# Splitting the second product of a conditional residual kernel differently: one matmul per sample and half instead of three per pair and half

## The chip, the cores and the metric

The kernel runs on one core of a Trainium2 chip. Its time is the device time of that core in microseconds (us). Of the kernel before there are three timed runs, and one profiled execution from which the trace comes.

## The reference

```python
x = x + einsum('bct,bcd->bdt', x, L0_cond_weights[itok_B_0_15])     # 64 x 64 per sample
x = x + einsum('bsi,boi->bso', x, L1_cond_weight[itok_B_3_7])       # 1024 x 1024 per sample
```

x is 128 samples of 64 x 1024 in float32. The first index picks one of 16 matrices W0 of 64 x 64, the second one of 8 adapters of 1024 x 1024 (the indices drawn are 3 to 7, so five adapters are used). Both steps are of the form (1 + W) applied to x, from the left and from the right, so they can be done in either order.

## The kernel before

The kernel does the large product first, z = x (1 + W1), and then y = (1 + W0) z. Two samples of one adapter make a pair of 128 rows, and a pair is one **slot**; an adapter with an odd number of samples has a last slot with one sample. There are 66 slots, numbered s, in groups of one adapter each. A table made on the chip says which samples, which W0s and which adapter a slot has.

Numbers are kept in fp32r, a rounded float32 that TensorE multiplies at full rate, and every factor is split into hi (the rounded value) and lo (what the rounding dropped), so that a product takes three matmuls: hi by hi, hi by lo, lo by hi. A slot has these steps:

- x is loaded by 8 DMAs (queue of SP), and VectorE (DVE) turns its 32 x 32 blocks (`turn_x`, L794). ScalarE (ACT) makes xt_hi (L572), DVE xt_lo (L803). In a slot with one sample, xt_hi holds hi in one half and lo in the other (L807).
- TensorE (PE) sums z in two halves of 512 columns, each half 8 tiles by 3 matmuls of 512 columns (`sum_z`, L467, L468, L470). Slots use the banks z_ps and first_ps by turns.
- ACT makes z_hi of a half (L584), DVE z_lo (L819), each 128 x 512.
- PE makes y of a half with 3 matmuls (`sum_y`, L481 to L483) whose stationary matrix is a block-diagonal w0_parts: W0 of sample A in one corner (put there by ACT, L580), W0 of sample B in the other (put there by DVE, L815). A slot with one sample uses w0_twice instead (L579).
- ACT copies y out of PSUM (L589) and issues the stores (L596).

The adapter of the next group is brought in meanwhile: it consists of 8 chunks of 128 rows, and the first 8 slots of a group handle one chunk each. A chunk is loaded, gets the identity added on GpSimd (L275), is turned by DVE (L779), and ACT and DVE make w_hi (L568) and w_lo (L789) of it. I call a slot with such a chunk a chunk slot and the others free slots. There are four groups that fetch a next one, hence 32 chunk slots.

Every engine has its own program, a loop over slots, and the engines meet at semaphores. In PE's program the y of slot s-1 stands between the two halves of z of slot s. ACT and DVE work strictly in the order of their programs. In DVE's program a slot s is, before the change:

```python
turn_x(j + h, 1 - h)        # x of slot s+1
keep_xt_lo(s + 1, 1 - h)    # waits for ACT's xt_hi, which waits for turn_x
turn_chunks(first, last)    # a chunk: turn, wait for ACT's w_hi, w_lo
keep_z_lo(s, h, 0)
place_w0_b(s)
keep_z_lo(s, h, 1)
```

`look` (L206) loads fields of the slot's row of the table into registers, on the engine that needs them.

## Time and profile before

| | us |
|---|---|
| median of 3 runs (lowest, highest) | 830.72 (828.99, 831.37) |
| profiled execution, its own time | 828.85 |
| its span | 827.1 |
| PE busy | 808.9 (98%) |
| DVE busy | 448.7 (54%) |
| ACT busy | 279.2 (34%) |
| GpSimd busy | 23.4 (3%) |

PE's matmuls are pipelined: each row of one lasts 0.39 us, but a new one starts every 0.227 us. Busy is the time in which at least one instruction of an engine runs. The time outside the span, 1.75 us, belongs to the start and the end of the execution. The trace also has rows for the sequencers (PEq, DVEq, ACTq), which do the loads into registers, the branches and the waits.

### The profile page before, as it was taken

What the parts mean: (1) busy time and instruction counts of PE and PEld (TensorE: products, weight loads), DVE (VectorE), ACT (ScalarE), POOL (GpSimd) and SP (SyncE); (2) the same over time, 40 slices, a digit from 0 to 9 for tenths busy, and PEclk for the clock granted to TensorE, in tenths of its full rate; (3) what the DMA queues carried; (4) which work ended last, traced back from release to release, by engine and by line L of the source; (5) the groups of instructions that cost most, each with busy time, mean ns of one, the idle gap of its engine ahead of it and who ended that gap; (6) DMA issues with size and microseconds to landing.
All of it is one profiled execution on the core that took longest, in us unless ns stands there. A gap on an engine that the chain in (4) does not pass through costs nothing.

```text
span 827.1 us, 17869 instructions
## 1 busy us (share of the span) xinstructions
PE 808.9 (98%) x3580; PEld 669.5 (81%) x3581; DVE 448.7 (54%) x472; ACT 279.2 (34%) x515; POOL 23.4 (3%) x60
## 2 busy tenths in 40 slices
PE   4999999999999999999999999999999999999998
PEld 4888888788888888888888888888888888888886
DVE  6666666566765434666663466665443343343342
ACT  3323424333333323424333233333332332332232
POOL 1100000010000000000000000000000000000000
PEclk9999999999999999999999999999999999999999
DMA  6344343444433324444333444433332233232232
GB/s 212 105 119 151 121 140 96 126 128 139 138 104 88 98 79 121 124 146 122 109 101 83 119 122 145 129 106 95 93 101 61 89 94 83 77 101 78 75 101 76
DMA packets 73952, 90.88 MB, mean 110 GB/s; under 512 B 13780, under 2 KB 64468, under 8 KB 73940
## 3 DMA queue, kind: packets, MB, share of 16 engines
q1 hardware_dynamic: 63616, 57.45, 23.2%
q10 hardware_dynamic: 10324, 33.30, 15.2%
q14 instruction: 8, 0.07, 0.0%
q8 instruction: 4, 0.07, 0.0%
HBM read 57.15 MB, written 33.55 MB: 110 GB/s over the span
## 4 chain that ended last, share of the span: by engine, by line
PE 82%; DVE 5%; issue 2%; ACT 2%; DVEq 2%; ACTq 1%; SPq 1%; DMA 1%; POOL 0%; POOLq 0%
PE z_ps L467 12%; PE first_ps L467 12%; PE z_ps L468 12%; PE first_ps L468 12%; PE z_ps L470 12%; PE first_ps L470 11%; PE y_ps L481 3%; PE y_ps L482 3%; PE y_ps L483 3%; DVE w_turned L779 2%; DVE x_turned L794 2%; DVEq L206 1%; ACT xt_hi L572 1%; ACT w_hi L568 1%; DMA w_nat<-in_L_cond_weight_dram 1%
## 5 line engine op out<-in xcount | busy, mean ns | idle before, releaser
L467 PE MATMUL z_ps<-w_hi,xt_hi 128*128 (+1 forms) x528 | 205.6, 389 | 0.5 <-DVE xt_lo L803 0.5
L468 PE MATMUL z_ps<-w_lo,xt_hi 128*128 (+1 forms) x528 | 205.4, 389 | 0.0
L467 PE MATMUL first_ps<-w_hi,xt_hi 128*128 x528 | 205.4, 389 | 0.0
L468 PE MATMUL first_ps<-w_lo,xt_hi 128*128 x528 | 205.4, 389 | 0.0
L470 PE MATMUL z_ps<-w_hi,xt_lo 128*128 (+1 forms) x512 | 199.2, 389 | 0.0
L470 PE MATMUL first_ps<-w_hi,xt_lo 128*128 x480 | 186.7, 389 | 0.0
L794 DVE STREAM_TRANSPOSE x_turned<-x_in 128x1024 f32<-128x1024 f32 x66 | 141.5, 2144 | 26.2 <-issue 23.3
L572 ACT ACTIVATE xt_hi<-x_turned 128x1024 fp32r<-128x1024 f32 x66 | 70.0, 1061 | 234.1 <-DVE x_turned L794 229.1
L803 DVE TENSOR_TENSOR xt_lo<-x_turned,xt_hi 128x1024 fp32r<-128x1024 f32 x61 | 74.8, 1225 | 78.4 <-ACT xt_hi L572 78.4
L467 PEld LDWEIGHTS z_ps<-w_hi,xt_hi 128*128 128x128 f32 x528 | 99.1, 188 | 21.7 <-issue 0.9
L467 PEld LDWEIGHTS first_ps<-w_hi,xt_hi 128*128 128x128 f32 x528 | 99.1, 188 | 20.7
L468 PEld LDWEIGHTS first_ps<-w_lo,xt_hi 128*128 128x128 f32 x528 | 99.1, 188 | 20.3
L468 PEld LDWEIGHTS z_ps<-w_lo,xt_hi 128*128 128x128 f32 x528 | 99.1, 188 | 20.3
L470 PEld LDWEIGHTS z_ps<-w_hi,xt_lo 128*128 128x128 f32 x512 | 96.1, 188 | 20.1
L470 PEld LDWEIGHTS first_ps<-w_hi,xt_lo 128*128 128x128 f32 x480 | 90.1, 188 | 18.8
L819 DVE TENSOR_TENSOR z_lo<-z_ps,z_hi 128x512 fp32r<-128x512 f32 x66 | 45.5, 689 | 89.3 <-ACT z_hi L584 88.0
L819 DVE TENSOR_TENSOR z_lo<-first_ps,z_hi 128x512 fp32r<-128x512 f32 x66 | 45.5, 689 | 88.4 <-ACT z_hi L584 88.0
L789 DVE TENSOR_TENSOR w_lo<-w_turned,w_hi x32 | 39.3, 1227 | 72.7 <-ACT w_hi L568 72.7
L568 ACT ACTIVATE w_hi<-w_turned x32 | 34.0, 1062 | 123.1 <-DVE w_turned L779 123.1
L589 ACT ACTIVATE y<-y_ps 128x512 f32<-128x512 f32 x130 | 70.2, 597 | 0.0
L779 DVE STREAM_TRANSPOSE w_turned<-w_nat 128x1024 f32<-128x1024 f32 x32 | 68.3, 2134 | 0.4 <-POOL w_nat L275 0.4
L584 ACT ACTIVATE z_hi<-z_ps 128x512 fp32r<-128x512 f32 x66 | 39.1, 593 | 84.9 <-PE z_ps L470 68.0
(137 smaller groups left out, 418.0 us busy)
## 6 DMA issues: line engine op xcount, KB each, us to landing
x_in<-in_x_dram SPq DMA_DIRECT2D x536, 64.0 KB, 2.0
out_dram<-y ACTq DMA_DIRECT2D x126, 256.0 KB, 3.1
w_nat<-in_L_cond_weight_dram SPq DMA_DIRECT2D x128, 128.0 KB
w_nat<-in_L_cond_weight_dram SPq DMA_DIRECT2D x4, 512.0 KB, 5.5
w_turned<-in_L_cond_weight_dram SPq DMA_DIRECT2D x2, 512.0 KB, 5.9
y<-in_L_cond_weight_dram SPq DMA_DIRECT2D x2, 512.0 KB, 8.1
x_turned<-in_L_cond_weights_dram SPq DMA_DIRECT2D x2, 256.0 KB, 4.0
x_in<-in_x_dram SPq DMA_DIRECT2D x2, 256.0 KB, 6.3
```

The source lines that it names most:

```text
L467: nc.tensor.matmul(to, xt_hi[h][:, t, :], whi, start=(t == 0), stop=False)
L468: mm = nc.tensor.matmul(to, xt_hi[h][:, t, :], wlo, start=False, stop=last and not pair)
L470: mm = nc.tensor.matmul(to, xt_lo[h][:, t, :], whi, start=False, stop=last)
L568: nc.scalar.activation(of_chunk(w_hi, k), turned(k), ACT.Copy).then_inc(chunk_hi_made, 1)
L572: nc.scalar.activation(xt_hi[h][:], x_turned[h][:], ACT.Copy).then_inc(xt_hi_made, 1)
L584: nc.scalar.activation(z_hi[:, n], z_banks[h][n][:], ACT.Copy).then_inc(z_hi_made, 1)
L589: nc.scalar.activation(y[h][:, n * HALF:(n + 1) * HALF], y_ps[n][:], ACT.Copy).then_inc(y_made, 1)
L779: nc.vector.transpose(w_turned[:, q].rearrange("p (t b m) -> p b t m", b=BLOCKS, m=BLOCK), w_nat[:, q].rearrange("p (b m t) -> p b t m", b ...
L789: nc.vector.tensor_tensor(of_chunk(w_lo, k), turned(k), of_chunk(w_hi, k).bitcast(F32), ALU.subtract).then_inc(chunk_lo_made, 1)
L794: nc.vector.transpose(x_turned[h][:].rearrange("p t (b m) -> p b t m", m=BLOCK), x_in[h][:].rearrange("p (b m t) -> p b t m", b=BLOCKS, m= ...
L803: nc.vector.tensor_tensor(xt_lo[h][:], x_turned[h][:], xt_hi[h][:].bitcast(F32), ALU.subtract).then_inc(xt_lo_made, 1)
L819: nc.vector.tensor_tensor(z_lo[:, n], z_banks[h][n][:], z_hi[:, n].bitcast(F32), ALU.subtract).then_inc(z_lo_made, 1)
```

## The change

z's hi and lo parts of one sample are stacked over the 128 partitions, and W0's hi and lo parts are set side by side as 128 columns, so that a single matmul of a sample and a half gives all the products. Its result has the part of W0's hi in 64 rows and that of W0's lo in the other 64, and these two are added afterwards: ACT copies one over to the other's partitions, DVE adds. The banks of y double from two to four, and one pair of start-up banks goes. DVE's slot is put in another order: the chunk is turned first, beside x, and x of slot s+2 is turned between the two halves.

```diff
-        w0_parts = sb("w0_parts", [P, 2, P], F32R)
-        w0_twice = sb("w0_twice", [P, 2, C], F32R)
-        z_hi = sb("z_hi", [P, NH, HALF], F32R)
-        z_lo = sb("z_lo", [P, NH, HALF], F32R)
+        w0_parts = sb("w0_parts", [P, 2, 2 * C], F32R)
+        z_parts = sb("z_parts", [P, NH, 2, HALF], F32R)
...
-        y_ps = [bank(f"y_ps{n}") for n in range(NH)]
+        y_ps = [[bank(f"y_ps{n}{k}") for k in range(2)] for n in range(NH)]
...
@@ SP, at the start @@
-            for c in range(6):
+            for c in range(4):
                 load_first(c)
-            sp.wait_ge(table_made, 1)
+            sp.wait_ge(samples_made, 1)
...
@@ PE @@
             def sum_y(s, pair):
...
                 for n in range(NH):
-                    pe.wait_ge(z_lo_made, NH * s + n + 1)
-                    to = y_ps[n][0:rows]
-                    nc.tensor.matmul(to, w0_slot[:, 0], z_hi[:, n], start=True, stop=False)
-                    nc.tensor.matmul(to, w0_slot[:, 0], z_lo[:, n], start=False, stop=False)
-                    nc.tensor.matmul(to, w0_slot[:, 1], z_hi[:, n], start=False, stop=True).then_inc(y_summed, 1)
+                    for k in range(2):
+                        pe.wait_ge(w0_placed, 2 * s + k + 1)
+                        pe.wait_ge(z_lo_made, PER_Z * s + 2 * n + k + 1)
+                        mm = nc.tensor.matmul(y_ps[n][k if pair else 0][:], w0_parts[:, k], z_parts[:, n, k],
+                                              start=pair or k == 0, stop=pair or k == 1)
+                        mm.then_inc(y_summed, 1)
...
                     if not second:
-                        pe.wait_ge(y_made, NH * before)
+                        pe.wait_ge(y_made, PER_Y * before)
                     sum_y(before, pair)
...
@@ ACT @@
             def keep_z_hi(s, h, n):
                 act.wait_ge(z_summed, NH * s + n + 1)
-                nc.scalar.activation(z_hi[:, n], z_banks[h][n][:], ACT.Copy).then_inc(z_hi_made, 1)
+                for k in range(2):
+                    nc.scalar.activation(z_parts[rows_of(k), n, k], z_banks[h][n][rows_of(k)],
+                                         ACT.Copy).then_inc(z_hi_made, 1)
+
+            def place_w0(s):
+                for k, cond in enumerate(look(act, s, COND_A, COND_B)):
+                    nc.scalar.activation(w0_parts[:, k], own_w0(cond), ACT.Copy).then_inc(w0_placed, 1)
+
+            def begin_y(s, h, stored):
+                act.wait_ge(y_stored[h], stored + STORED_AHEAD)
+                def across(k, n, count):
+                    act.wait_ge(y_summed, PER_Y * s + 2 * n + 2)
+                    nc.scalar.activation(y[h][rows_of(k), n * HALF:(n + 1) * HALF], y_ps[n][k][rows_of(1 - k)],
+                                         ACT.Copy).then_inc(y_begun, count)
+                stores, = look(act, s, STORES)
+                with act.If(stores > 1):
+                    for n in range(NH):
+                        for k in range(2):
+                            across(k, n, 1)
+                with act.Else():
+                    for n in range(NH):
+                        across(0, n, 2)
...
             def slot(j, h, before, stored):
...
                 keep_z_hi(s, h, 0)
-                make_y(before, 1 - h)
-                place_w0_a(s)
+                act.wait_ge(y_summed, PER_Y * before + 4)
+                place_w0(s)
+                begin_y(before, 1 - h, stored)
                 keep_z_hi(s, h, 1)
                 store_y(before, 1 - h)
...
@@ DVE @@
             def keep_z_lo(s, h, n):
-                dve.wait_ge(z_hi_made, NH * s + n + 1)
-                nc.vector.tensor_tensor(z_lo[:, n], z_banks[h][n][:], z_hi[:, n].bitcast(F32), ALU.subtract).then_inc(z_lo_made, 1)
+                for k in range(2):
+                    dve.wait_ge(z_hi_made, PER_Z * s + 2 * n + k + 1)
+                    nc.vector.tensor_tensor(z_parts[rows_of(1 - k), n, k], z_banks[h][n][rows_of(k)],
+                                            z_parts[rows_of(k), n, k].bitcast(F32), ALU.subtract).then_inc(z_lo_made, 1)
+
+            def finish_y(s, h):
+                def add(k, n, begun, count):
+                    dve.wait_ge(y_begun, PER_Y * s + begun)
+                    own = y[h][rows_of(k), n * HALF:(n + 1) * HALF]
+                    nc.vector.tensor_tensor(own, y_ps[n][k][rows_of(k)], own, ALU.add).then_inc(y_made, count)
...
-            def slot(j, h):
+            def slot(j, h, before):
                 s = 2 * j + h
                 first, last = look(dve, s, CHUNKS_BEFORE, CHUNKS)
-                turn_x(j + h, 1 - h)
+                with dve.If(last > first):
+                    turn_chunk(first)
                 keep_xt_lo(s + 1, 1 - h)
-                turn_chunks(first, last)
+                with dve.If(last > first):
+                    keep_chunk_lo(first)
+                with dve.If(last > first + 1):
+                    with dve.Fori(first + 1, last) as k:
+                        turn_chunk(k)
+                        keep_chunk_lo(k)
                 keep_z_lo(s, h, 0)
-                place_w0_b(s)
+                finish_y(before, 1 - h)
+                turn_x(j + 1, h)
                 keep_z_lo(s, h, 1)
```

On DVE, from the first z_lo of a slot in the loop to the turning of the next x, this stood before:

```order
L819 TENSOR_TENSOR z_lo<-z_ps,z_hi 128x512
L206 ISA
L206 TENSOR_LOAD slot_row
L815 ISA
L815 COPY w_parts<-w_all 64x2x64
L818 REGISTER_ALU
L819 TENSOR_TENSOR z_lo<-z_ps,z_hi 128x512
L206 ISA
L206 TENSOR_LOAD slot_row
L793 ISA
L794 STREAM_TRANSPOSE x_turned<-x_in 128x4x8x32
```

From the same place, up to the second of four sums of y, DVE now has:

```order
L808 TENSOR_TENSOR z_parts<-z_ps,z_parts 64x512
L807 REGISTER_ALU
L808 TENSOR_TENSOR z_parts<-z_ps,z_parts 64x512
L205 ISA
L205 TENSOR_LOAD slot_row
L819 COMPARE_AND_BRANCH
L814 ISA
L816 TENSOR_TENSOR y<-y_ps,y 64x512
L814 REGISTER_ALU
L816 TENSOR_TENSOR y<-y_ps,y 64x512
```

Each z_lo has become two instructions on 64 partitions, the copy of W0 has left DVE, and a load of a field, a branch and four sums of y have come between the z_lo of the first half and the turning of x, which for its part stands ahead of the z_lo of the second half.

On PE, the y of a slot with two samples was this:

```order
L481 MATMUL y_ps<-z_hi,w_parts 128x512
L482 MATMUL y_ps<-z_lo,w_parts 128x512
L483 MATMUL y_ps<-z_hi,w_parts 128x512
L481 MATMUL y_ps<-z_hi,w_parts 128x512
L482 MATMUL y_ps<-z_lo,w_parts 128x512
L483 MATMUL y_ps<-z_hi,w_parts 128x512
```

It is now this, in the same place between the halves of z:

```order
L479 MATMUL y_ps<-z_parts,w_parts 128x512
L477 REGISTER_ALU
L478 REGISTER_ALU
L479 MATMUL y_ps<-z_parts,w_parts 128x512
L478 REGISTER_ALU
L479 MATMUL y_ps<-z_parts,w_parts 128x512
L478 REGISTER_ALU
L479 MATMUL y_ps<-z_parts,w_parts 128x512
```

Six matmuls of 512 columns have become four of 512 columns, and each of the four waits for a z_lo of its own.

## Rows read from the trace of the kernel before

**Rows 1.** Part 1 of the page: busy time of each engine.
```profile
PE 808.9 (98%) x3580; PEld 669.5 (81%) x3581; DVE 448.7 (54%) x472; ACT 279.2 (34%) x515; POOL 23.4 (3%) x60
```

**Rows 2.** Waits of PE: line, waited for, us in total, times, longest.
```profile
PE first_ps L448 <- DMA x_in<-in_x_dram: 3.4, 1, 3.4
...
PE z_ps L467 <- DVE xt_lo L803: 0.5, 1, 0.5
```

**Rows 3.** Stretches: busy us (instructions) of each engine, granted clock, DMA.
```profile
22.00:24.00 2.00, 1.64 (x8) 1.64 (x9) 0.00 (x0) 0.49 (x1) 1.36 (x6) 0.50 0.86 311
...
574.30:821.00 246.70, 246.70 (x1090) 203.96 (x1089) 99.31 (x102) 73.84 (x145) 0.00 (x0) 1.00 0.32 85
```

**Rows 4.** DVE's turnings of chunks, line L779: durations, and busy tenths in 40 slices.
```profile
L779 DVE STREAM_TRANSPOSE w_turned<-w_nat x32: 2112/2130/2161, 46.0 to 562.0; 128x1024 f32<-128x1024 f32 x32
...
busy tenths in 40 slices 0021221012111000221210022111000000000000
```

**Rows 5.** DVE in order of time, one chunk slot and parts of its neighbours.
```profile
411.93 0.68 DVE L819 TENSOR_TENSOR z_lo<-first_ps,z_hi 128x512 fp32r<-128x512 f32 x1
412.64 0.23 DVE L815 CAST w_parts<-w_all 64x128 fp32r x1
412.97 0.69 DVE L819 TENSOR_TENSOR z_lo<-first_ps,z_hi 128x512 fp32r<-128x512 f32 x1
414.29 2.15 DVE L794 STREAM_TRANSPOSE x_turned<-x_in 128x1024 f32<-128x1024 f32 x1 [0.63 <-issue]
417.57 1.23 DVE L803 TENSOR_TENSOR xt_lo<-x_turned,xt_hi 128x1024 fp32r<-128x1024 f32 x1 [1.13 <-ACT xt_hi L572]
418.71 2.12 DVE L779 STREAM_TRANSPOSE w_turned<-w_nat 128x1024 f32<-128x1024 f32 x1
423.03 1.23 DVE L789 TENSOR_TENSOR w_lo<-w_turned,w_hi  x1 [2.20 <-ACT w_hi L568]
424.17 0.68 DVE L819 TENSOR_TENSOR z_lo<-z_ps,z_hi 128x512 fp32r<-128x512 f32 x1
...
425.21 0.69 DVE L819 TENSOR_TENSOR z_lo<-z_ps,z_hi 128x512 fp32r<-128x512 f32 x1
426.00 2.15 DVE L794 STREAM_TRANSPOSE x_turned<-x_in 128x1024 f32<-128x1024 f32 x1
```

**Rows 6.** ACT in order of time, in the same slot.
```profile
421.36 1.06 ACT L568 ACTIVATE w_hi<-w_turned  x1 [3.83 <-DVE w_turned L779]
...
422.80 1.08 ACT L589 ACTIVATE y<-y_ps 128x512 f32<-128x512 f32 x2
...
423.96 0.30 ACT L580 ACTIVATE w_parts<-w_all 64x128 fp32r x1
```

**Rows 7.** Two neighbours on DVE without a change of partitions.
```profile
133.12 0.69 DVE L807 TENSOR_TENSOR xt_hi<-x_turned,xt_hi 128x512 fp32r<-128x512 f32 x1 [1.13 <-ACT xt_hi L572]
133.73 2.16 DVE L779 STREAM_TRANSPOSE w_turned<-w_nat 128x1024 f32<-128x1024 f32 x1
```

**Rows 8.** DVE's loads of table fields into registers: durations in ns, min/median/max.
```profile
L206 DVEq TENSOR_LOAD <-slot_row x198: 300/318/1864, 20.8 to 816.0; - x198
```

**Rows 9.** Slot 1: PE's first matmul; DVE's first chunk turned.
```profile
39.10 0.39 PE L467 MATMUL first_ps<-w_hi,xt_hi 128*128 x1
...
46.05 2.13 DVE L779 STREAM_TRANSPOSE w_turned<-w_nat 128x1024 f32<-128x1024 f32 x1 [0.35 <-POOL w_nat L275]
```

**Rows 10.** The end, in order of time: PE's last z, then ACT and DVE.
```profile
820.86 0.39 PE L470 MATMUL first_ps<-w_hi,xt_lo 128*128 x1
...
821.28 0.60 ACT L584 ACTIVATE z_hi<-first_ps 128x512 fp32r<-128x512 f32 x1 [4.07 <-PE first_ps L470]
...
821.91 0.69 DVE L819 TENSOR_TENSOR z_lo<-first_ps,z_hi 128x512 fp32r<-128x512 f32 x1 [5.08 <-ACT z_hi L584]
...
823.19 0.69 DVE L859 COPY y<-y_ps 128x512 f32<-128x512 f32 x1 [0.59 <-PE y_ps L542]
```

More of the change, by code:

```diff
@@ L183, in conditional_residual_kernel @@
         w0_lo_made = sem("w0_lo_made")
-        w0_placed = [sem(f"w0_placed{k}") for k in range(2)]
+        w0_placed = sem("w0_placed")
         z_summed = sem("z_summed")
@@ L359, in _ @@
                 sp.dma_start(x_in[0][k * C:(k + 1) * C, :], x_rows[bass.ds(sample * C, C), :]).then_inc(x0_loaded, 16)
-            for c in range(6, CHUNKS_PER_GROUP):
+            for c in range(4, CHUNKS_PER_GROUP):
                 load_first(c)
@@ L530, in y_last @@
             def y_last(pair):
-                pe.wait_ge(y_made, 4 * pairs_past + 2)
-                s = 2 * pairs_past + 1
-                for k in range(2):
-                    pe.wait_ge(w0_placed[k], s + 1)
-                w0_slot, rows = (w0_parts, P) if pair else (w0_twice, C)
-                for n in range(NH):
-                    to = y_ps[n][0:rows]
-                    pe.wait_ge(z_hi_made, NH * s + n + 1)
-                    nc.tensor.matmul(to, w0_slot[:, 0], z_hi[:, n], start=True, stop=False)
-                    nc.tensor.matmul(to, w0_slot[:, 1], z_hi[:, n], start=False, stop=False)
-                    pe.wait_ge(z_lo_made, NH * s + n + 1)
-                    nc.tensor.matmul(to, w0_slot[:, 0], z_lo[:, n], start=False, stop=True).then_inc(y_summed, 1)
+                pe.wait_ge(y_made, PER_Y * (2 * pairs_past + 1))
+                sum_y(2 * pairs_past + 1, pair)
             for_both(stores, y_last)
@@ L598, in store_y @@
                 with act.If(stores > 1):
-                    act.wait_ge(y_made, NH * s + NH)
+                    act.wait_ge(y_made, PER_Y * s + PER_Y)
                     store(a, 0)
@@ L607, in store_y, with slot @@
                     with act.Else():
-                        act.wait_ge(y_made, NH * s + NH)
+                        act.wait_ge(y_made, PER_Y * s + PER_Y)
                         act.sem_inc(y_stored[h], 32)
-            def slot(j, h, before, last_of_all=False):
+            def slot(j, h, before, stored):
                 s = 2 * j + h
@@ L771, in keep_x0_lo, with turn_chunk, turn, keep_chunk_lo @@
                     keep(slice(C, P), xt_hi[0])
-            def turn_chunks(first, last):
-                with dve.If(last > first):
-                    with dve.Fori(first, last) as k:
-                        def turn(q):
-                            dve.wait_ge(chunk_with_1, k + 1)
-                            nc.vector.transpose(
-                                w_turned[:, q].rearrange("p (t b m) -> p b t m", b=BLOCKS, m=BLOCK),
-                                w_nat[:, q].rearrange("p (b m t) -> p b t m", b=BLOCKS, m=BLOCK)
-                                ).then_inc(chunk_turned, 1)
-                        with dve.If(k % 2 < 1):
-                            turn(0)
-                        with dve.Else():
-                            turn(1)
-                        dve.wait_ge(chunk_hi_made, k + 1)
-                        nc.vector.tensor_tensor(of_chunk(w_lo, k), turned(k), of_chunk(w_hi, k).bitcast(F32),
-                                                ALU.subtract).then_inc(chunk_lo_made, 1)
+            def turn_chunk(k):
+                def turn(q):
+                    dve.wait_ge(chunk_with_1, k + 1)
+                    nc.vector.transpose(
+                        w_turned[:, q].rearrange("p (t b m) -> p b t m", b=BLOCKS, m=BLOCK),
+                        w_nat[:, q].rearrange("p (b m t) -> p b t m", b=BLOCKS, m=BLOCK)
+                        ).then_inc(chunk_turned, 1)
+                with dve.If(k % 2 < 1):
+                    turn(0)
+                with dve.Else():
+                    turn(1)
+            def keep_chunk_lo(k):
+                dve.wait_ge(chunk_hi_made, k + 1)
+                nc.vector.tensor_tensor(of_chunk(w_lo, k), turned(k), of_chunk(w_hi, k).bitcast(F32),
+                                        ALU.subtract).then_inc(chunk_lo_made, 1)
             def turn_x(j, h):
@@ L821, in slot @@
-            def slot(j, h):
+            def keep_z_lo(s, h, n):
+                for k in range(2):
[7 more added lines that the diff above has]
+                    nc.vector.tensor_tensor(own, y_ps[n][k][rows_of(k)], own, ALU.add).then_inc(y_made, count)
+                stores, = look(dve, s, STORES)
+                with dve.If(stores > 1):
+                    for n in range(NH):
+                        for k in range(2):
+                            add(k, n, 2 * n + k + 1, 1)
+                with dve.Else():
+                    for n in range(NH):
+                        add(0, n, 2 * n + 2, 2)
```

95 lines of the change are left out of this document (34 added, 61 removed).

## The prediction

> **What bounds the kernel now.** First the busy shares [rows 1]: PE is busy 98% of the span, the next engine, DVE, 54%. Then PE's waits [rows 2]: behind the start there is one, 0.5 us long, for DVE's xt_lo. Then the pace [rows 3]: in the undisturbed stretch at the end PE starts 1090 matmuls in 246.7 us, one per 0.2263 us, at full granted clock. So the time is the number of matmuls of 512 columns by 0.2265 us: a slot has 48 of z and 6 of y, 54 x 0.2265 = 12.23 us.
>
> The average of 54% on DVE hides two sorts of slots. In a chunk slot DVE goes from one turning of x (414.29) to the next (426.00) in 11.7 us, and from z_lo at 411.93 to z_lo at 424.17 in 12.24 us, with next to no spare time [rows 5]: of this it waits 1.13 us for xt_hi and 2.20 us for w_hi, answers from ACT that come only after its own turnings. The wait of PE for xt_lo stands at the end of the first series of 8 such slots. The chunk slots come in four series of 8, 32 turnings [rows 4]. DVE is thus already a near second bound in them, and the change adds to DVE.
>
> **PE, what it saves.** y of a slot takes 4 matmuls where it took 6, for pairs and for single samples alike, with the same 512 columns and, since the stationary matrix still has 128 columns, the same pace. All 66 slots: 396 become 264. I count the last slot in the tail; the other 65 save 130 x 0.2265 = **29.4 us**. A slot needs 52 x 0.2265 = 11.78 us of PE.
>
> **ACT, what it gets.** Two more passes of z_hi and two more of y, each 0.49 us behind another (1.08 us for two [rows 6]), so some 2 us a slot on an engine that is busy a third of the time [rows 1]. Cover: in a chunk slot ACT sits idle 3.83 us before w_hi [rows 6]. Without the cover it would cost up to 2 us in each slot. I take 0. Its stores are issued behind the last of y as before.
>
> **DVE, what it gets.** Gone: the copy of W0, 0.23 us. Added in a pair slot: two z_lo passes and four sums of y, all of 512 columns, 0.69 us each, since half the partitions save nothing: the copy of 64 partitions [rows 5] is short by its 128 columns. In the new order xt_lo needs no wait, as its x was turned in the slot before, and it fills 1.2 us of the 2.2 us in which DVE waits for w_hi. Laid end to end from the start of the last z_lo of a chunk slot to that of the next:
>
> - to the turning of the chunk: 0.79 us in the first slot of the loop's body and 1.32 us past the loop's end [rows 5], mean 1.05, and two more branches and a wait, for which I put 0.2: 1.25
> - from the turning to w_lo: 4.32 [rows 5], xt_lo inside it
> - w_lo to z_lo: 1.14 overlapped as before, 1.26 if it may not overlap: 1.26
> - z_lo to z_lo 0.72, z_lo to the first sum of y 0.72 (the load of one field, 0.32 [rows 8], lies beside), three more sums 2.16, last sum to the turning of x 0.72
> - the turning of x to z_lo 2.18, z_lo to z_lo 0.72
>
> Sum **14.05 us**, against 11.78 us of PE. The spacing of the seven short steps is the choice that matters. A pass of 0.69 us is followed after 0.61 us in one place [rows 7], and after 0.71 us in the other, where the next one begins at another partition (z_lo, then the copy to rows 64 on [rows 5]). Nearly every new instruction changes between rows 0 and 64 in what it reads or writes, so I take 0.72. At 0.61 throughout, with 1.14 for w_lo and without the 0.2, the chain is 12.9 us; with 0.1 more on each step for register work it is 14.9 us.
>
> The Trainium skill has a rule on this (VectorE: DVE Perf Modes, section "Two Vector instructions with no wait between them"): an instruction whose inputs or output start in another quadrant of partitions than those before is held until everything earlier has finished. By that rule every z_lo, every sum of y and both turnings here are held, which is the chain of 14.05 us; without it the sum would come out at 828 us as in the second case below. The two spacings agree with it.
>
> **How far DVE may fall behind.** In free slots PE sets the pace. The end of z gives the offsets [rows 10]: last matmul starts at 820.86, so PE is through at E = 821.08; z_hi starts at E+0.2, z_lo at E+0.83. In the new order DVE is by then still turning x: ACT makes z_hi twice, two W0s and four copies, so the last sum of y ends at about E-0.5, the turning at E+1.6, and the second z_lo starts at E+2.3. PE needs it at E + 24 + 3 matmuls = E+6.1, minus 0.75 for the pass: E+5.3. Slack: **3.0 us**. A chunk slot uses up 14.05 - 11.78 = 2.27 us of it, and what remains is a wait of PE before y. It isn't won back, since in free slots PE can do no better than 11.78.
>
> - Series 2 to 4: 8 x 2.27 - 3.0 = 15.2 us each, 45.5 us. The free slots between (at least two) give DVE some 1.8 us each, enough to restore the slack.
> - Series 1 starts without slack: DVE turns the first chunk at 46.05, when it has landed, with slot 1 on PE since 39.10 [rows 9], some 0.5 earlier after. From there 4.32+1.26+0.72+0.72+2.16+0.72+2.18+0.72 brings the second z_lo to 58.9, needed at 38.6 + 11.78 + 5.3 = 55.7: 3.2 late, and 7 more slots by 2.27: 19.1 us. The 0.5 us of before [rows 2] goes into this.
>
> **Start.** x of slot 0 is asked for ahead of two chunks instead of behind. PE waited 3.4 us for it [rows 2]. The bytes ahead of the last chunk are the same, and PE would wait for chunks next: between 0 and 3.4, I take 0.5 us of gain, near the lower end because of the DMA load in that stretch [rows 3].
>
> **Tail.** Before, the last copy on DVE starts 2.1 us after E [rows 10]. After: z_lo twice (E+0.83 and 1.5), the last matmul at E+2.2, its end 0.4 later, two copies on ACT of 0.6 and 0.5, the last sum at E+4.0: **+1.9 us**.
>
> **Sum**, against the profiled execution's own 828.85 us: - 29.4 - 0.5 (start) - 0.5 (old wait) + 45.5 + 19.1 + 1.9 = 865.0. The median of the runs is 1.9 us above that execution; I halve that and say **866 us**.
>
> **The rivals.**
> 1. DVE's steps overlap, chain 12.9 us. For it: [rows 7]. Series 2 to 4 cost 8 x 1.12 - 3.0 = 6.0 each, series 1 2.3 + 7 x 1.12 = 10.1: 28.1 in all, 828 us, no change. With chains from 12.3 to 13.4 us this case spans 809 to 844.
> 2. Faster: DVE keeps pace. The place is the wait for w_hi: if ACT's answer came while xt_lo runs, turning to w_lo would be 2.13 + 1.23 = 3.4 us instead of 4.32, and the chain 11.95 us with overlap. That is below the 12.15 us from which 8 slots use up the slack. Only some 3 us of series 1 stay: 803 us. Against it: ACT starts w_hi 0.5 us after the turning ends, needs 1.06, and DVE starts 0.6 later [rows 5, 6]. The change is a gain at all only below a chain of some 12.9 us.
> 3. Worse: a wait not in the chain (sums of y waiting for ACT's copies, loads into registers, the longest of which took 1.86 us [rows 8]), chain 15 us or more: 895 us.
>
> TensorE's clock is no case of its own. After the 3.4 us wait for x the granted clock was 0.50, its 1.2 GHz level [rows 2, 3]. PE's new waits are some 2.3 us a slot, and should the clock fall nonetheless, what the slower matmuls lose comes out of PE's wait for DVE.
>
> **How the numbers follow.** Forecast (chains of 13.4 to 14.9 us, 844 to 892) 0.67, rival 1 0.18, rival 2 0.10, rival 3 0.05. The range that leaves out rival 2, the lower end of rival 1 and the top is 826 to 884. A measurement here tells 0.3%, 2.5 us, from no change. Faster: rival 2 and a third of rival 1, 0.16; same 0.05; slower 0.79.
>
> **What would show it.** Right: four blocks of PE waits for z_lo inside the series of 8, some 2.3 us a slot from the second slot on, none in free slots; DVE near 100% busy or waiting for w_hi there, slots of 14 us; y at 4 matmuls of 0.2265; DVE busy about 66 x 3.9 us more. Wrong: PE waits in free slots, or for y_made, or waits for w_hi of under 0.5 us, or PE without waits at a span near 800.

## The result, and the profile after

The changed kernel took **858.25 us** (median of four executions, 857.83 to 859.58), the kernel before 831.05 us on the same chip (828.99 to 831.84). The ratio is 1.0327, with a 95% interval of 1.031 to 1.0343: 3.3% slower. The profiled execution of the changed kernel took 859.58 us, with a span of 857.6; before it was 828.85 with a span of 827.1. So there are 30.5 us to find inside the span. In all that follows one execution stands apart: of the ten of the kernel with the new order and the old y, one took 1674.46 us and the others 829.93 to 831.99, and its ratio leaves that one out.

Part 1 of the changed kernel's page is the counterpart of [rows 1]:

```profile
PE 806.3 (94%) x3448; PEld 644.7 (75%) x3449; DVE 706.1 (82%) x795; ACT 453.3 (53%) x771; POOL 23.7 (3%) x59
```

132 matmuls are gone, and yet PE is busy for only 2.6 us less: a matmul that is held up by the next one's input is drawn longer than its 0.23 us, so part of the waiting hides in "busy". DVE has gained 257 us, which is 66 slots by 3.9 us. At 82% it still doesn't look like a bound; the average is over slots with and without a chunk.

PE's waits, the counterpart of [rows 2]:

```profile
PE y_ps L479 <- DVE z_parts L808: 30.5, 54, 1.9
...
PE y_ps L448 <- DMA x_in<-in_x_dram: 1.3, 1, 1.3
PE y_ps L479 <- DVE y L816: 0.9, 2, 0.6
```

Where before there was one wait of 0.5 us behind the start, there are now 54 waits before y for z_lo (L808), and two for sums of y. Nearly all stand where the chunks are turned (DVE's L771, the counterpart of [rows 4]: its first and last start, and in which of the 40 slices it is busy):

```profile
L771 DVE STREAM_TRANSPOSE w_turned<-w_nat x32: 2120/2186/2242, 47.1 to 595.1; 128x1024 f32<-128x1024 f32 x32
...
busy tenths in 40 slices 0021212021212000112120011212000000000000
```

How long a slot is, I read from PE's starts, from the first matmul after one y to the first after the next. Before, it was 12.24 us in every slot of two samples, but for the one wait. Now it is 11.78 to 11.79 us in most slots without a chunk, and 13.5 to 13.7 us in those with one, apart from the first one or two of a series (15.39 us in the first series, where the chunk comes late, and 11.8 to 12.3 us in the others, where the slack is used up first). Here is one slot with a chunk on DVE, in order of time, to be laid beside [rows 5] (start, duration, line, operation, count, and in brackets the idle time before it and who ended it):

```profile
390.83 2.15 DVE L771 STREAM_TRANSPOSE w_turned<-w_nat 128x1024 f32<-128x1024 f32 x1
392.91 1.18 DVE L797 TENSOR_TENSOR xt_lo<-x_turned,xt_hi 128x1024 fp32r<-128x1024 f32 x1
395.25 1.23 DVE L783 TENSOR_TENSOR w_lo<-w_turned,w_hi  x1 [1.16 <-ACT w_hi L555]
396.51 1.41 DVE L808 TENSOR_TENSOR z_parts<-z_ps,z_parts 64x512 fp32r<-64x512 f32 x2
397.95 2.85 DVE L816 TENSOR_TENSOR y<-y_ps,y 64x512 f32<-64x512 f32 x4
400.83 2.13 DVE L788 STREAM_TRANSPOSE x_turned<-x_in 128x1024 f32<-128x1024 f32 x1
403.00 1.41 DVE L808 TENSOR_TENSOR z_parts<-z_ps,z_parts 64x512 fp32r<-64x512 f32 x2
404.43 2.17 DVE L771 STREAM_TRANSPOSE w_turned<-w_nat 128x1024 f32<-128x1024 f32 x1
```

From turning to turning it is 404.43 - 390.83 = 13.60 us; over the seven steps of the first series it is (142.66 - 47.14)/7 = 13.65. Only the 1.16 us before w_lo are idle, and not one instruction of this slot waits for PE. PE for its part, at the start of this stretch, waits for the z_lo of the slot before: its second half has two, which DVE starts at 389.39 and 390.11, and PE waits for each:

```profile
388.70 0.61 PE L479 MATMUL y_ps<-z_parts,w_parts 128*128 128x512 f32 x2
390.13 0.50 PE L479 MATMUL y_ps<-z_parts,w_parts 128*128 128x512 f32 x1 [0.82 <-DVE z_parts L808]
390.86 0.49 PE L479 MATMUL y_ps<-z_parts,w_parts 128*128 128x512 f32 x1 [0.22 <-DVE z_parts L808]
391.37 0.49 PE L467 MATMUL z_ps<-w_hi,xt_hi 128*128 x1
```

From 388.70 to 391.37 four matmuls take 2.67 us; at the usual pace they would take 0.91. The brackets show only 1.04 of this loss, since the ends of the held matmuls are drawn late. So the list of waits (30.5 us) understates the loss, and I count by starts.

**The books of the span, before to after:**

| where | predicted, us | measured, us |
|---|---|---|
| y with four matmuls for six | -29.4 | -29.0 (64 slots by 0.453) |
| old wait for xt_lo, and start | -1.0 | -0.8 |
| first series of chunks | +19.1 | +20.3 |
| waits in the other three | +45.5 | +35.0 (11.8, 11.6, 11.7) |
| behind single-sample slots | 0 | +1.0 |
| tail | +1.9 | +4.1 |
| sum | +36.1 | +30.6, of 30.5 |

A row's loss is what its slots take beyond 11.785 us (9.98 where a slot has one sample).

Not all of the 20.3 us are waits. Behind the last chunk slot of the first series comes a slot in which PE waits for nothing, and still it takes 1.7 us too long. In it eight matmuls start 0.43 us apart instead of 0.227, because the granted clock is down at 0.50, the 1.2 GHz level (PE, PEld, DVE, ACT, GpSimd, then the clock, DMA's share and GB/s):

```profile
158.00:161.00 3.00, 3.00 (x9) 2.35 (x8) 2.88 (x5) 2.68 (x6) 0.00 (x0) 0.50 0.32 89
```

PE had lost 3.7 us in the slot before. In the kernel below whose sums have 256 columns, where the clock stays at 1.00, the same slot loses 0.6 us, so the fall costs here at least 1.1 us, by my estimate.

### The profile page after: what moved, and what is told of

It reads as the page before. It is cut to its first block, busy times and chain, and to the rows that moved or that the text cites. A ratio compares the mean times of both kernels' runs of the same rounds, so it can differ in the third digit from the quotient of the medians.

```text
span 857.6 us, 19195 instructions
## 1 busy us (share of the span) xinstructions
PE 806.3 (94%) x3448; PEld 644.7 (75%) x3449; DVE 706.1 (82%) x795; ACT 453.3 (53%) x771; POOL 23.7 (3%) x59
## 4 chain that ended last, share of the span: by engine, by line
PE 40%; DVE 22%; issue 17%; DVEq 10%; ACT 5%; ACTq 2%; DMA 2%; SPq 1%; POOL 0%; POOLq 0%
DVE w_turned L771 8%; DVE z_parts L808 8%; PE z_ps L467 6%; PE first_ps L467 6%; PE z_ps L470 6%; PE z_ps L468 6%; PE first_ps L468 6%; DVEq L205 5%; PE first_ps L470 5%; DVE y L816 5%; ACT w_hi L555 4%; PE y_ps L479 3%; DVEq L783 2%; ACTq L555 2%; DMA y<-in_L_cond_weight_dram 1%
## 5 line engine op out<-in xcount | busy, mean ns | idle before, releaser
L467 PE MATMUL first_ps<-w_hi,xt_hi 128*128 x528 | 208.2, 394 | 0.3
L816 DVE TENSOR_TENSOR y<-y_ps,y 64x512 f32<-64x512 f32 x256 | 176.0, 689 | 16.8 <-ACT y L577 9.7
L577 ACT ACTIVATE y<-y_ps 64x512 f32<-64x512 f32 x256 | 150.7, 590 | 7.5 <-PE y_ps L479 2.5
L788 DVE STREAM_TRANSPOSE x_turned<-x_in 128x1024 f32<-128x1024 f32 x67 | 143.5, 2142 | 2.0
L479 PE MATMUL y_ps<-z_parts,w_parts 128*128 128x512 f32 x264 | 87.1, 416 | 31.7 <-DVE z_parts L808 30.5
L468 PEld LDWEIGHTS first_ps<-w_lo,xt_hi 128*128 128x128 f32 x528 | 99.7, 189 | 20.3
L564 ACT ACTIVATE z_parts<-z_ps 64x512 fp32r<-64x512 f32 x132 | 78.2, 592 | 44.7 <-PE z_ps L470 31.2
L564 ACT ACTIVATE z_parts<-first_ps 64x512 fp32r<-64x512 f32 x132 | 78.2, 593 | 43.7 <-PE first_ps L470 29.3
L808 DVE TENSOR_TENSOR z_parts<-z_ps,z_parts 64x512 fp32r<-64x512 f32 x132 | 90.9, 689 | 9.2 <-ACT z_parts L564 5.3
L808 DVE TENSOR_TENSOR z_parts<-first_ps,z_parts 64x512 fp32r<-64x512 f32 x132 | 90.9, 689 | 9.0 <-ACT z_parts L564 5.2
```

The source lines that it names most:

```text
L467: nc.tensor.matmul(to, xt_hi[h][:, t, :], whi, start=(t == 0), stop=False)
L468: mm = nc.tensor.matmul(to, xt_hi[h][:, t, :], wlo, start=False, stop=last and not pair)
L479: mm = nc.tensor.matmul(y_ps[n][k if pair else 0][:], w0_parts[:, k], z_parts[:, n, k], start=pair or k == 0, stop=pair or k == 1)
L564: nc.scalar.activation(z_parts[rows_of(k), n, k], z_banks[h][n][rows_of(k)], ACT.Copy).then_inc(z_hi_made, 1)
L577: nc.scalar.activation(y[h][rows_of(k), n * HALF:(n + 1) * HALF], y_ps[n][k][rows_of(1 - k)], ACT.Copy).then_inc(y_begun, count)
L788: nc.vector.transpose(x_turned[h][:].rearrange("p t (b m) -> p b t m", m=BLOCK), x_in[h][:].rearrange("p (b m t) -> p b t m", b=BLOCKS, m= ...
```

## The experiments

The theory: in a slot with a chunk, DVE's steps laid end to end (the chain, 13.65 us) are longer than PE's 11.79, and after some 3 us of slack each such slot costs PE the difference. The rivals: a wait or register work that the list of steps doesn't hold, or the new order of DVE's slot. All kernels from here on except the changed one itself carry this addition in `look`, by which the values loaded from the table are kept in bounds:

```diff
-            return values
+            return tuple(eng.snap(v & (TOP[f] | 7), min_val=0, max_val=TOP[f]) if f in (GROUP, CHUNKS_BEFORE, CHUNKS) else v
+                         for f, v in zip(range(fields[0], fields[-1] + 1), values))
```

**The addition alone**, on the changed kernel. It adds register instructions ahead of DVE's turnings, so it is a test of the register rival too.

> The changed kernel, with the table's chunk and group fields masked to their range (value & 63, value & 7) after each load: what the runs below are compared with. One or two register operations more for each load of these fields. If DVE's sequencer has time to spare beside the passes, as the chain theory has it (the steps behind the loads follow without a gap in the changed kernel's trace, 0.72 us from z_lo to the turning of the chunk), the slot stays at 13.65 us and the time at 858 us within 2. If register work is what sets the chain, each of 31 slots gets some 0.1 us longer: 861 us or more.

Measured: 859.51 us (856.76 to 860.24), ratio 1.0325 (1.030 to 1.0351). The chain stayed at 13.63 to 13.66 us (the mean of each series), and the turning of the chunk still starts 0.72 us after the last z_lo. More register work there costs nothing that can be measured: it runs while the pass before it does. This kernel is the base for the experiments below.

**Less of each sum of y.** The four sums stay four instructions but get fewer columns, 256 or 64 for 512. The rest of y is left out.

```diff
-                    own = y[h][rows_of(k), n * HALF:(n + 1) * HALF]
-                    nc.vector.tensor_tensor(own, y_ps[n][k][rows_of(k)], own, ALU.add).then_inc(y_made, count)
+                    own = y[h][rows_of(k), n * HALF:n * HALF + 256]
+                    nc.vector.tensor_tensor(own, y_ps[n][k][rows_of(k), 0:256], own, ALU.add).then_inc(y_made, count)
```

> The four sums of y take 256 of their 512 columns; the other columns of the output lack the part of one of W0's halves. Chain theory: a pass of 256 columns is 0.27 us shorter, the chain of a chunk slot 13.65 - 1.07 = 12.58 us, PE loses 8 x 0.80 - 3.3 = 3.1 us in series 2 to 4 and about 9 in series 1: 55 - 18 = 37 us less, about 822. Rival, the hand-over between PE, ACT and DVE costs PE the time (each wait a matter of latency, not of DVE's work): the number of hand-overs is unchanged, 855 to 860.

> The four sums of y take 64 of their 512 columns; the rest of the output's columns lack one part. Chain theory: 0.47 us less on each of four passes, chain 11.8 us, as long as PE's slot: only the late start of series 1 (some 3 us) stays, 806 us, PE without waits elsewhere. Rival, hand-overs: 855 to 860 as before. If the sums' fixed cost is larger than I think, between 806 and 822.

Measured, with one execution each: 824.18 us and 809.18 us. DVE's row for the four sums and PE's waits, with 256 columns, then with 64:

```profile
390.13 1.78 DVE L816 TENSOR_TENSOR y<-y_ps,y 64x256 f32<-64x256 f32 x4
...
PE y_ps L479 <- DVE z_parts L808: 5.5, 8, 1.8
```

```profile
392.08 1.01 DVE L816 TENSOR_TENSOR y<-y_ps,y 64x64 f32<-64x64 f32 x4
...
PE y_ps L479 <- DVE z_parts L808: 3.4, 7, 1.1
```

The group of four shrinks from 2.85 to 1.78 us, and the slots with a chunk from 13.65 to between 12.4 and 12.6 us. With 64 columns all slots are 11.79 us from the second series on: PE is the bound there. Of the 3.4 us of waits that are left, 2.0 are in the first series and 1.4 behind the last z. Nothing but DVE's time was touched, and 50 us went. That shows the theory's main step. It also shows that 808 us is about what the four-matmul y is worth once DVE isn't in its way.

**The old order of DVE's slot, with the new y.** The new order could itself be the cause.

```diff
             def slot(j, h, before):
...
-                with dve.If(last > first):
-                    turn_chunk(first)
+                turn_x(j + h, 1 - h)
                 keep_xt_lo(s + 1, 1 - h)
                 with dve.If(last > first):
-                    keep_chunk_lo(first)
-                with dve.If(last > first + 1):
-                    with dve.Fori(first + 1, last) as k:
+                    with dve.Fori(first, last) as k:
                         turn_chunk(k)
                         keep_chunk_lo(k)
                 keep_z_lo(s, h, 0)
                 finish_y(before, 1 - h)
-                turn_x(j + 1, h)
                 keep_z_lo(s, h, 1)
...
             keep_z_lo(0, 0, 0)
-            turn_x(1, 0)
             keep_z_lo(0, 0, 1)
```

> The new y with DVE's old order of a slot (x turned first, then xt_lo, then the chunk). Chain theory: the two waits for ACT no longer share the time of other work. Chain = 2.15 + 1.13 (turning of x, wait for xt_hi) + 1.14 + 4.4 (to w_lo) + 1.26 + 6 passes by 0.72 + 0.72 to the last z_lo's end + looks 0.3 = about 15.9 us, PE loses 31 x 4.1 less the slack, 115 to 125 us: about 920. Rival, the new order itself is what costs: about 830 or less.

Measured: 922.69 us, in one execution. DVE in a slot with a chunk:

```profile
396.43 1.22 DVE L797 TENSOR_TENSOR xt_lo<-x_turned,xt_hi 128x1024 fp32r<-128x1024 f32 x1 [1.13 <-ACT xt_hi L559]
397.57 2.14 DVE L771 STREAM_TRANSPOSE w_turned<-w_nat 128x1024 f32<-128x1024 f32 x1
401.93 1.23 DVE L783 TENSOR_TENSOR w_lo<-w_turned,w_hi  x1 [2.22 <-ACT w_hi L555]
```

and PE's waits:

```profile
PE y_ps L479 <- DVE y L816: 57.9, 29, 2.8
PE y_ps L479 <- DVE z_parts L808: 6.1, 24, 0.9
```

The two waits of DVE for ACT from [rows 5] are back at their old lengths, and its slots are 15.5 to 15.9 us. PE mostly waits for the sums of y now (L816, `y_made`) and not for z_lo: a DVE that is later still frees y's banks too late. The new order isn't the cause; it saves 63 us of what the new y would cost without it.

**The new order, with the old y.** The same order in the kernel before, whose y stays at six matmuls.

```diff
             def slot(j, h):
...
-                turn_x(j + h, 1 - h)
+                with dve.If(last > first):
+                    turn_chunk(first)
                 keep_xt_lo(s + 1, 1 - h)
-                turn_chunks(first, last)
+                with dve.If(last > first):
+                    keep_chunk_lo(first)
+                with dve.If(last > first + 1):
+                    with dve.Fori(first + 1, last) as k:
+                        turn_chunk(k)
+                        keep_chunk_lo(k)
                 keep_z_lo(s, h, 0)
...
+                turn_x(j + 1, h)
                 keep_z_lo(s, h, 1)
```

> The kernel before with DVE's new order alone (chunk turned first, x of slot s+2 turned between the halves), y as before. Chain theory: PE sets the pace at 12.24 us a slot, DVE has more time to spare than before, and the one wait of PE at the end of series 1 (0.8 us) goes: 829 to 831 us, no change that can be told. Rival, the new order is itself harmful: 833 or more.

Measured: 831.69 us, ratio 0.9994 (0.9982 to 1.0006). The old wait of PE for xt_lo (0.5 us in the list, 0.8 by starts) is gone, every slot of two samples is 12.24 us, and the time is the same. Room on an engine that isn't the bound brings nothing by itself.

**Sums that stay on their partitions.** This weighs the spacing of DVE's passes, which the prediction called the choice that matters. In the changed kernel each z_lo and each sum begins at another partition than the pass before, in what it reads or in what it writes. Here the sums of y go in the order (n,k) = (0,0), (1,0), (1,1), (0,1), so two of the three neighbour pairs among them keep their rows.

```diff
-                    for n in range(NH):
-                        for k in range(2):
-                            add(k, n, 2 * n + k + 1, 1)
+                    for n, k in [(0, 0), (0, 1), (1, 0), (1, 1)] if last else [(0, 0), (1, 0), (1, 1), (0, 1)]:
+                        add(k, n, 2 * n + k + 1, 1)
```

> The four sums of y in the order A, B, B, A instead of A, B, A, B, so that one of the three changes of rows between neighbours goes. The first sum follows a z_lo that read rows 64 on, so it and both changes stay. If a change of the starting partition keeps the next pass from overlapping, one step of 0.72 becomes 0.61 in each chunk slot: 31 x 0.11 = 3.4 us less, 855 to 856. If 0.72 is the spacing of such passes whatever their rows (reading PSUM, waiting on a register), 859 as after_masked. The row of the trace that tells it is the start-to-start time of the second and the third sum.

Measured: 852.44 us (851.19 to 853.2), ratio 1.0256 (1.0229 to 1.0283), 7.1 us below its base; the two intervals lie apart. The four sums as one row:

```profile
392.52 2.62 DVE L816 TENSOR_TENSOR y<-y_ps,y 64x512 f32<-64x512 f32 x4
```

The row that tells is the start-to-start time: 0.61, 0.70 and 0.62 us between these four, where the changed kernel has 0.71 to 0.73 three times. Together they take 2.62 us for 2.85, that is 0.23 for two pairs or 0.11 for one; the slots with a chunk went from 13.65 to 13.40 us. 32 slots with a chunk by 0.23 are 7.4 us. The expectation above describes the order with one such pair where the kernel has two, and so names half of the effect. For one pair 3.5 us would have been right. The size of the effect for each pair is what it assumed (0.72 against 0.61).

**Taking the remaining wait out of the chain.** DVE idles 1.16 us for ACT's w_hi in each of these slots. Here z_hi and z_lo of the first half go ahead of w_hi and w_lo, on ACT and on DVE.

```diff
@@ ACT, slot @@
-                keep_chunks_hi(first, last)
...
                 keep_z_hi(s, h, 0)
+                keep_chunks_hi(first, last)
...
@@ DVE, slot @@
                 keep_xt_lo(s + 1, 1 - h)
+                keep_z_lo(s, h, 0)
                 with dve.If(last > first):
                     keep_chunk_lo(first)
...
-                keep_z_lo(s, h, 0)
                 finish_y(before, 1 - h)
```

> z_hi of the first half ahead of w_hi on ACT, z_lo of the first half ahead of w_lo on DVE, so that DVE does these two passes while ACT makes w_hi. Chain theory: the wait for w_hi and the register work behind it (1.16 us of idle in each chunk slot) goes, chain 2.08 + 1.26 + 1.44 + 1.26 + 2.88 + 2.17 + 1.44 = 12.5 us, PE loses some 19 us instead of 55: 822 us. Rival, it is the number of passes alone that counts and idle time on DVE elsewhere takes its place: 855 to 859.

Measured: 828.77 us (827.57 to 830.07), ratio 0.9968 (0.9956 to 0.998). DVE:

```profile
384.83 2.19 DVE L770 STREAM_TRANSPOSE w_turned<-w_nat 128x1024 f32<-128x1024 f32 x1
386.95 1.18 DVE L796 TENSOR_TENSOR xt_lo<-x_turned,xt_hi 128x1024 fp32r<-128x1024 f32 x1
388.16 1.41 DVE L807 TENSOR_TENSOR z_parts<-first_ps,z_parts 64x512 fp32r<-64x512 f32 x2
389.60 1.23 DVE L782 TENSOR_TENSOR w_lo<-w_turned,w_hi  x1
```

The idle time is gone and the chain is 12.50 us, as expected. The time is 7 us above what was expected all the same. In the second series PE lost 4.9 us where 8 x (12.50 - 11.79) = 5.7 were over, so the slack was only 0.8 us, and not the 3.3 us of the changed kernel (8 x 1.87 - 11.7). Series 2 to 4 together lost 14.4 us where 3 x (5.7 - 3.3) = 7.2 were to be expected, so the miss lies in them. The trace shows where the slack went: from the first turning of each of these series to the second it is 14.2 to 14.3 us, against 12.5 to 12.7 for the steps behind it. I read it so: w_lo, 1.26 us, now stands behind a z_lo that can't begin before PE has ended the half, so it can no longer be done in advance. How much earlier DVE may be is a price of its own, beside the length of its chain. That w_lo's place is the reason is argued; no run tests it alone.

**w_lo on GpSimd.** GpSimd is busy 3% of the span. It gets the subtraction of the chunk, right behind its own step for that chunk, and DVE's turning waits for it only as far back as the buffer needs.

```diff
@@ POOL, add_1_to_chunks, behind the step of a chunk @@
+                        pool.wait_ge(chunk_hi_made, k + 1)
+                        nc.gpsimd.tensor_tensor(of_chunk(w_lo, k), turned(k), of_chunk(w_hi, k).bitcast(F32),
+                                                ALU.subtract).then_inc(chunk_lo_made, 1)
@@ DVE, turn_chunk @@
+                    dve.wait_ge(chunk_lo_made, k + (CHUNKS_PER_GROUP - 1))
@@ DVE @@
-            def keep_chunk_lo(k):
...
                 with dve.If(last > first):
-                    turn_chunk(first)
-                keep_xt_lo(s + 1, 1 - h)
-                with dve.If(last > first):
-                    keep_chunk_lo(first)
-                with dve.If(last > first + 1):
-                    with dve.Fori(first + 1, last) as k:
+                    with dve.Fori(first, last) as k:
                         turn_chunk(k)
-                        keep_chunk_lo(k)
+                keep_xt_lo(s + 1, 1 - h)
```

> w_lo of the chunks is made by GpSimd, which is idle, and DVE waits for it no more. Chain theory: DVE's chunk slot loses the wait and the pass, 13.65 - 4.34 + 2.08 - 1.26 + 1.26 = 11.4 us, below PE's 11.78: only the late start of series 1 and the single-sample slot stay, 806 to 811 us. Rival: GpSimd is slow at it (its 128-column addition takes 0.46 to 0.51 us, so 1024 columns may take 4 us) and passes of DVE that overlap with it are held up: 815 to 835, with longer xt_lo or turnings in the trace.

Measured: 826.16 us (824.02 to 827.86), ratio 0.9938 (0.9913 to 0.9963), where 806 to 811 was expected. The chain fell to 12.57 us and no further. The row on DVE, and the pass on GpSimd in the same slot:

```profile
385.29 1.41 DVE L807 TENSOR_TENSOR z_parts<-first_ps,z_parts 64x512 fp32r<-64x512 f32 x2 [1.15 <-ACT z_parts L567]
```

```profile
385.18 2.40 POOL L325 TENSOR_TENSOR w_lo<-w_turned,w_hi  x1 [9.72 <-ACT w_hi L558]
```

DVE's wait for ACT hasn't gone, it has changed its name: 1.15 us for z_hi, which on ACT stands behind w_hi. Here is ACT in that slot:

```profile
383.58 1.06 ACT L558 ACTIVATE w_hi<-w_turned  x1 [2.33 <-DVE w_turned L775]
384.67 1.21 ACT L567 ACTIVATE z_parts<-first_ps 64x512 fp32r<-64x512 f32 x2
```

ACT idles for 2.33 us until the chunk is turned, and only then makes w_hi and z_hi. The pass itself was moved at no cost to DVE. What runs beside it are z_lo and the sums of y, and they take 0.69 us each, with it or without it. Both read one operand from PSUM. None of DVE's passes with both inputs in SBUF (xt_lo) falls into GpSimd's pass in any of these kernels, so whether such a pass would be held up stays open.

**Both together**: w_lo on GpSimd, and on ACT z_hi of the first half ahead of w_hi.

> w_lo on GpSimd and, on ACT, z_hi of the first half ahead of w_hi. In w_lo_on_gpsimd DVE sat idle 1.15 us in each chunk slot because z_lo waited for a z_hi that ACT makes only behind w_hi; that wait goes. Chain theory: 2.08 + 1.21 + 1.44 + 2.88 + 2.17 + 1.44 = 11.2 us, perhaps 0.2 more where the sums wait for ACT, below PE's 11.78: PE waits only for the late first chunk and at the single-sample slot, some 4 us in all, about 808 us. Rival: GpSimd's pass of 2.4 us and DVE's passes hold each other up, or ACT's order makes the sums wait: chain above 11.78 again, 815 to 828.

Measured: **808.70 us** (806.57 to 810.54), ratio **0.9737** (0.9709 to 0.9765). This beats the kernel before by 2.6% and the changed one by 5.8%. Part 1 of its page, DVE in one slot, and PE's waits:

```profile
PE 781.8 (97%) x3448; PEld 643.4 (80%) x3449; DVE 666.5 (83%) x763; ACT 450.6 (56%) x771; POOL 97.6 (12%) x91
```

```profile
381.15 2.17 DVE L774 STREAM_TRANSPOSE w_turned<-w_nat 128x1024 f32<-128x1024 f32 x1 [0.28 <-issue]
...
384.46 1.41 DVE L806 TENSOR_TENSOR z_parts<-z_ps,z_parts 64x512 fp32r<-64x512 f32 x2
386.18 2.85 DVE L814 TENSOR_TENSOR y<-y_ps,y 64x512 f32<-64x512 f32 x4 [0.31 <-ACT y L580]
...
392.70 2.17 DVE L774 STREAM_TRANSPOSE w_turned<-w_nat 128x1024 f32<-128x1024 f32 x1
```

```profile
PE y_ps L482 <- DVE z_parts L806: 2.8, 5, 1.9
```

The slots with a chunk are 11.79 us from the second series on. In the first series the first is 13.15 us, and the others of two samples are 11.8 to 12.0. DVE's share of the span is no lower than in the changed kernel (83% against 82%), but in the slots that count its chain has dropped below PE's 11.79 us. GpSimd's part alone brought 33 of the 51 us against its base, and ACT's order on top of it the other 17.

**Two more savings on top of that**: the sums on their own partitions as above, and the last round of the loop written out, so that DVE doesn't turn an x there that nobody uses.

```diff
                 finish_y(before, 1 - h)
-                turn_x(j + 1, h)
+                if turns:
+                    turn_x(j + 1, h)
...
-            with dve.Fori(0, pairs_past) as i:
+            but_one = dve.snap((pairs_past - 1) & 63, min_val=0, max_val=MOST_PAIRS - 2)
+            with dve.Fori(0, but_one) as i:
...
-            finish_y(2 * pairs_past + 1, 1)
+            slot(but_one + 1, 0, 2 * but_one + 1)
+            slot(but_one + 1, 1, 2 * but_one + 2, turns=False)
+            finish_y(2 * pairs_past + 1, 1, last=True)
```

> As z_first_gpsimd, with the sums in the order A, A, B, B (two neighbours on the same rows) and without the turning of an x that no slot uses, which in the last slot stands ahead of the last z_lo. DVE isn't the bound any more, so the order of the sums gives nothing; the turning that goes lets the last z_lo start some 1 us earlier. 807 us, 0.970 of the kernel before.

Measured: 811.01 us (809.62 to 811.48), ratio 0.9752 (0.9729 to 0.9775). Its interval overlaps that of the kernel before it (0.9709 to 0.9765), so no gain is shown, and the expectation is missed. DVE and the last z_lo:

```profile
380.32 2.02 DVE L814 TENSOR_TENSOR y<-y_ps,y 64x512 f32<-64x512 f32 x3 [0.55 <-ACT y L580]
...
800.12 1.41 DVE L806 TENSOR_TENSOR z_parts<-first_ps,z_parts 64x512 fp32r<-64x512 f32 x2 [0.75 <-ACT z_parts L567]
```

Both savings turn into waits for ACT. The second sum now needs the third of ACT's copies. The last z_lo, freed of the turning, starts 1.0 us sooner behind PE's last z in spite of its wait of 0.75 us for z_hi, and nothing comes of it: the end of the span lies 10.0 us behind the end of PE's last z here, as in the kernel before it. What holds the end is ACT (the end of PE's last z is at 799.29):

```profile
800.52 1.13 ACTq L597 DMA_DIRECT2D out_dram<-y  x2
...
801.58 0.50 PE L482 MATMUL y_ps<-z_parts,w_parts 128*128 128x512 f32 x1 [0.23 <-DVE z_parts L806]
803.10 2.44 ACT L580 ACTIVATE y<-y_ps 64x512 f32<-64x512 f32 x4 [2.40 <-issue]
```

ACT's four copies of y start 1.5 us after the last matmul did and wait for nothing. ACT's sequencer first issues the two stores of the slot before, and then loads a field of the table, 0.76 us from 802.15 on. The copies start 3.8 us behind the end of PE's last z in this kernel, and 3.8 to 3.9 in the changed one, in the one whose sums stay on their partitions and in the one with both moves, though the last z_lo of these four starts anywhere from 0.8 to 2.1 us behind that end.

PE's first z also came 2 us later (29.26 against 27.30 us), behind a wait of 1.9 us for x's DMA, and one early slot took 13.16 us, in which DVE's turning waits 1.47 us for GpSimd's step of the chunk; how much of that is the edit and how much differs between executions I can't tell.

## Why the prediction was right, and where its terms were off

The forecast was 866 us, range 826 to 884, slower at 0.79. Measured were 858.25 us and slower. It is the forecast case: four blocks of waits for z_lo, one for each series of 8 slots with a chunk, and nearly all other slots at 11.79 us. Of its signs of being wrong two showed, both small: PE waited twice for a sum of y, 0.9 us in all, and lost 1.0 us in free slots behind those with one sample.

1. **PE's saving** (-29.4): held, 0.453 us a slot. The slots without a chunk show it undisturbed.
2. **The chain** (14.05): measured 13.65. The spacing of 0.72 us between passes, its main choice, held throughout: 1.41 us for two, 2.85 for four, and the experiment on the sums shows that 0.11 of each is the change of rows. w_lo to z_lo took 1.26, as put down. Turning to w_lo took 4.42 for 4.32, w_lo again waiting for w_hi, which rival 2 had against it. The step that was mis-sized is the first one, "to the turning of the chunk", put at 1.25 us: measured 0.72 from the second z_lo to it, the spacing of any other such pass. The 0.79 and 1.32 us of [rows 5] were read there as the price of loads and branches, with 0.2 more for new ones. In the changed kernel the loads run while two z_lo passes, the branches too, and nothing is left over. The kernel with more register work agrees.
3. **Slack** (3.0): measured 3.3. With the shorter chain, 8 x 1.87 - 3.3 = 11.7 us a series, for the 15.2 forecast. The 0.4 us of chain are 9.6 of the 10.5 us by which the last three series were over-estimated.
4. **The first series** (19.1): measured 20.3, right in size by luck, through errors that cancel. The shorter chain takes 7 x 0.4 = 2.8 us off. The first slot lost 3.6 us instead of 3.2. The last one runs beside z of a slot with one sample, where PE has only some 10 us of work and DVE's chain is as long as ever, since the shorter xt pass is hidden behind the wait for w_hi: it lost 3.7 us instead of 1.9, where the prediction counted all slots alike. And the slot behind the series lost 1.7 us with the clock at 0.50. 19.1 - 2.8 + 0.4 + 1.9 + 1.7 = 20.3. The prediction had said that what slower matmuls lose would come out of PE's wait for DVE. Here it did not, as that slot had no such wait.
5. **Start** (-0.5 forecast, about 0 measured): PE's wait for x fell from 3.4 to 1.3 us, and it waited for chunks instead; z began 0.4 us later than before. The bound below, no gain at all, was the right one.
6. **Tail** (+1.9): measured +4.1. Here DVE in the changed kernel's last slot, with PE's last z ending at 847.47:

```profile
847.12 2.12 DVE L788 STREAM_TRANSPOSE x_turned<-x_in 128x1024 f32<-128x1024 f32 x1
849.27 1.41 DVE L808 TENSOR_TENSOR z_parts<-first_ps,z_parts 64x512 fp32r<-64x512 f32 x2
...
852.00 2.85 DVE L816 TENSOR_TENSOR y<-y_ps,y 64x512 f32<-64x512 f32 x4 [1.31 <-ACT y L577]
```

The turning at 847.12 is of an x that no slot uses, issued because the new order has it in the loop's body; it puts z_lo 1.0 us later than the 0.83 us behind z that was forecast. That isn't what costs the time, though: in the last experiment above the turning is gone, z_lo starts 0.83 us behind z and the last matmul 2.3 us, as forecast, and the tail is as long as before. The forecast had the first two of ACT's four copies done by then, so that two stood behind the last matmul. But ACT's sequencer issues the stores of the slot before and loads a field first, so all four copies start together, 3.9 us behind z, and after the first of them come four sums. The last begins at 854.1, 6.7 us behind z, for the forecast 4.0. The program lets the first copy go after two matmuls; it is ACT's own order that keeps it back.

The rivals: DVE's steps overlapping (chain 12.9) fell to the spacings; DVE keeping pace fell to the 1.16 us of waiting for w_hi in every slot; hidden waits (chain over 15) were not there. The mechanism of the second rival was a real one, though: once that wait and w_lo are out of DVE's way, the time is 809 us, against its 803.

## What to carry to other kernels

Before an engine gets more work, add up its instructions end to end in the stage where it has most to do, by spacings from the trace and with its waits for others, and compare that with the bound's time in the same stage; 54% on average hid a chain that was full. Halving the partitions of an instruction doesn't make it cheaper, so count instructions and columns when results are spread over more of them. And when a step is taken off a full engine, look at the program order of the engine that feeds it: a third of the gain lay in a z_hi that stood behind a w_hi, and the tail was set by stores and a load that ACT's program has ahead of its last copies.

## What the runs showed of the hardware

- A DVE pass that begins at other partitions than the one before it starts 0.72 us after that one's start, for 512 fp32 columns; one on the same partitions starts after 0.61. Keeping the rows in two of the three neighbour pairs of each slot's sums took 7.1 us off the whole. The Trainium skill (VectorE: DVE Perf Modes, section "Two Vector instructions with no wait between them") states the rule, that a pass which starts in another quadrant of partitions is held until the earlier ones have finished. The trace agrees, and these runs give the rule a price here: 0.11 us for each change.
- A pass of 512 fp32 columns takes DVE 0.69 us on 64 partitions (z_lo and the sums of y in the changed kernel) and on 128 (z_lo in the kernel before).
- Loads of fields into registers and branches on DVE had no price while a pass ran ahead of them: 0.72 us from the last z_lo to the next turning, with a load and branches between, and with masks added. With no pass ahead they had one: at the end ACT's copies waited for its stores and for a load of 0.76 us.
- A subtraction of 1024 fp32 columns took 2.40 us on GpSimd and 1.23 us on DVE. The passes of DVE that ran beside it, each with one operand in PSUM, were not longer for it (0.69 us).
- Losses of some 1.9 us in each slot with a chunk left TensorE's granted clock nearly untouched. It was 1.00, the 2.4 GHz level, over the stretch from 240 to 570 us, in which 17 chunks are turned. It fell to 0.50, the 1.2 GHz level, once among the slots, from 158 to 161 us, after PE had lost 3.7 us in one slot, and matmuls then started 0.43 us apart. Over the whole span it was 0.992. The old order, with waits of up to 2.8 us, came out at 0.96.
